# VectorE's ratio at the head of each step of the factor pipeline, and routing weights turned and expanded by short one-pass products

## The reference, cut to what matters

```python
# decay mixing, per batch and channel, over time
decay = exp(-exp(w)) * (0.5 + 0.5 * tf)            # tf from cond, one number per batch
ek, ekv = exp(min(k, 30)), exp(min(k, 30)) * v
nf, df = forward scans of ekv, ek  (a = a * decay + ekv_t; b = b * decay + ek_t)
nb, db = the same scans in reverse
euk = exp(min(u + k, 30))
y = sigmoid(x) * (nf + nb - ekv + euk * v) / max(df + db - ek + euk, 1e-8) * (0.8 + 0.2 * tf)
# routed low rank layer, per token
h = silu(y @ rw1.T + rb1);  logits = (h @ rw2.T + rb2)[:, :16] + gates
coeff = softmax over the two largest logits, at their places, else 0      # 16 experts
xa = y @ A.T                                        # 16 experts x rank 16 = 256
out = x + (y @ W.T + bias) + (xa * coeff[expert]) @ B
```

## Time and profile before

| | us |
|---|---|
| median of 3 runs | 688.93 (688.32 to 689.98) |
| the profiled execution's own time | 688.6 |
| its span, first to last instruction | 686.6 |
| TensorE busy | 598.7 (87%) |
| VectorE busy | 526.6 (77%) |
| GpSimd busy | 368.1 (54%) |
| ScalarE busy | 357.1 (52%) |

### The profile page before, as it was taken

One profiled execution on the slowest core, in us unless ns is written; L12 is line 12 of the kernel. 1 busy time (PEld: TensorE's weight loads), 2 busy tenths in 40 slices (PEclk: granted clock), 3 DMA queues, 4 the chain that ended last, 5 costly groups with the idle time before them and its releaser, 6 DMA issues.

```text
span 686.6 us, 7030 instructions
## 1 busy us (share of the span) xinstructions
PE 598.7 (87%) x2626; PEld 490.1 (71%) x2626; DVE 526.6 (77%) x573; ACT 357.1 (52%) x418; POOL 368.1 (54%) x183
## 2 busy tenths in 40 slices
PE   0153588989999937999999999999999999999997
PEld 0132466768878825887888878888888888888886
DVE  7999999999999999998899797979897532021202
ACT  4777789785656666655655554656465420011000
POOL 1789997867868876647544753565465501000100
PEclk9976799989999978999999999999999999999999
DMA  5323476522945831234423360427132402040022
GB/s 190 122 90 121 124 254 205 194 100 71 215 107 121 203 113 64 74 113 160 141 73 113 109 198 32 153 63 242 33 116 84 124 29 66 27 153 1 25 67 76
DMA packets 33169, 78.42 MB, mean 114 GB/s; under 512 B 4720, under 2 KB 4848, under 8 KB 33136
## 3 DMA queue, kind: packets, MB, share of 16 engines
q1 hardware_dynamic: 30832, 73.79, 33.2%
q0 software_dynamic: 2304, 4.20, 3.8%
HBM read 57.00 MB, written 20.97 MB: 114 GB/s over the span
## 4 chain that ended last, share of the span: by engine, by line
PE 49%; DVE 25%; POOL 16%; issue 7%; ACT 1%; DMA 1%; SPq 0%; DVEq 0%; POOLq 0%; ACTq 0%
PE acc L925 15%; PE acc L927 15%; PE acc L926 15%; DVE mix L713 5%; POOL mix L602 4%; POOL kv L580 4%; POOL yr L586 4%; DVE yr L747 3%; DVE mix L708 3%; DVE eu L723 3%; DVE kv L718 2%; DVE xo L754 2%; POOL y_lo L612 2%; DVE mix L734 2%; PE acc L936 1%
## 5 line engine op out<-in xcount | busy, mean ns | idle before, releaser
L925 PE MATMUL acc<-y_hi,wa_hi 128*128 128x512 f32 x640 | 258.5, 404 | 59.7 <-POOL y_lo L612 52.7
L926 PE MATMUL acc<-y_lo,wa_hi 128*128 128x512 f32 x640 | 255.3, 399 | 0.0
L927 PE MATMUL acc<-y_hi,wa_lo 128*128 128x512 f32 x640 | 254.8, 398 | 0.0
L925 PEld LDWEIGHTS acc<-y_hi,wa_hi 128*128 128x128 f32 x640 | 124.1, 194 | 89.3 <-POOL y_lo L612 54.1
L927 PEld LDWEIGHTS acc<-y_hi,wa_lo 128*128 128x128 f32 x640 | 123.8, 194 | 26.7
L926 PEld LDWEIGHTS acc<-y_lo,wa_hi 128*128 128x128 f32 x640 | 124.2, 194 | 25.6
L602 POOL TENSOR_TENSOR mix<-mix,kv 128x1024 f32<-128x1024 f32 x31 | 74.3, 2397 | 75.7 <-DVE mix L692 59.4
L754 DVE SCALAR_TENSOR_TENSOR xo<-acc,bias_sb,xo 128x512 f32<-128x512 f32 x64 | 46.4, 735 | 75.2 <-PE acc L927 75.2
L612 POOL TENSOR_TENSOR y_lo<-yr,y_hi 128x1024 fp32r<-128x1024 f32 x31 | 74.3, 2398 | 50.2 <-ACT y_hi L402 50.2
L625 POOL TENSOR_TENSOR wx_lo<-xa,wx_hi 128x512 fp32r<-128x512 f32 x16 | 20.9, 1329 | 129.3 <-ACT wx_hi L470 129.3
L580 POOL TENSOR_TENSOR kv<-mix,kv 128x1024 f32<-128x1024 f32 (+1 forms) x32 | 75.4, 2356 | 5.3 <-DVE mix L734 5.3
(11 more groups left out here) (98 smaller groups left out, 738.3 us busy)
## 6 DMA issues: line engine op xcount, KB each, us to landing
kv<-f_cm SPq DMA_DIRECT2D x32, 512.0 KB, 3.6
yr<-x_cm SPq DMA_DIRECT2D x32, 512.0 KB, 3.4
out<-xo SPq DMA_DIRECT2D x64, 256.0 KB, 4.2
xo<-x_cm SPq DMA_DIRECT2D x64, 256.0 KB, 3.9
out<-xo POOLq DMA_DIRECT2D x16, 256.0 KB, 6.8
xa<-w_base SPq DMA_DIRECT2D x5, 512.0 KB, 3.5
xo<-w_base SPq DMA_DIRECT2D x3, 512.0 KB, 5.7
xo<-w_router_a SPq DMA_DIRECT2D x2, 480.0 KB, 3.6
```

What stands on the lines that cost most here:

```text
L925: nc.tensor.matmul(out_ap, wh, yh, start=start, stop=False)
L926: nc.tensor.matmul(out_ap, wh, yl, start=False, stop=False)
L927: return nc.tensor.matmul(out_ap, wl, yh, start=False, stop=stop)
```

## The change

VectorE's `ratio` moves from the middle of a step to its head and multiplies the inverse with the sigmoid; GpSimd's `gate_n` then multiplies the summed numerator with that, and its result is y. GpSimd's sum is written over the numerator, so that the buffer of k is free sooner. ScalarE's order changes with it: `exp_uk` and `sigmoid_r` come to the head of the step. The groups 0 and 1 take the same places in a step as the later ones, with G = 1 in steps 11 to 13. The routing weights are no longer repeated to 512 columns: high and low parts of the 16 weights, twice side by side (`cat`, 64 columns), are turned by four fp32r products (`turn`), copied by ScalarE (`copy_turned`), and expanded to 128 rows by two products of 512 columns with a constant 0/1 matrix (`spread`). `ident` and `expand` are loaded into a free buffer and copied to fp32r by ScalarE in step 3 (`constants`). `u_g` and its copy go away; `split_wx` on GpSimd comes after `split_lo`.

```diff
+        cat = nc.alloc_sbuf_tensor_at("cat", [P, TPG, 2, 2 * E], fp32r, offset=fan_at)
+        cat_t = nc.alloc_sbuf_tensor_at("cat_t", [4 * E, N], fp32r, offset=fan_at + 4 * N)
+        ident_r = sb("ident_r", [P, P], fp32r)
+        expand_r = sb("expand_r", [4 * E, P], fp32r)
...
-        (AFTER_FWD, AFTER_FWD_NUM, AFTER_RATIO, AFTER_BWD_DEN, AFTER_P2, AFTER_SUM, AFTER_BWD_NUM) = range(7)
-        hidden_at = {(CB, AFTER_BWD_NUM): 0, (CB + 3, AFTER_SUM): 1}
-        silu_at = {(CB + 1, AFTER_FWD): 0, (CB + 3, AFTER_BWD_NUM): 1}
-        routing_at = {(CB + 1, AFTER_BWD_DEN): 0, (CB + 4, AFTER_FWD): 1}
-        weigh_at = {(CB + 1, AFTER_P2): 0, (CB + 4, AFTER_RATIO): 1}
...
+        (AFTER_RATIO, AFTER_FWD, AFTER_FWD_NUM, AFTER_BWD_DEN, AFTER_SUM, AFTER_BWD_NUM) = range(6)
+        evacs_at = {(CB + 2, AFTER_RATIO): (0, 1), (CB + 2, AFTER_FWD): (1, 3), (CB + 2, AFTER_FWD_NUM): (3, 5),
+                    (CB + 2, AFTER_BWD_DEN): (5, 6), (CB + 2, AFTER_BWD_NUM): (6, 7), (CB + 3, AFTER_RATIO): (7, 8),
+                    (CB + 4, AFTER_BWD_NUM): (8, 10), (CB + 5, AFTER_FWD): (10, 12), (CB + 5, AFTER_FWD_NUM): (12, 13),
+                    (CB + 5, AFTER_BWD_DEN): (13, 14), (CB + 5, AFTER_SUM): (14, 15),
+                    (CB + 5, AFTER_BWD_NUM): (15, 16)}
...
         def first_step(G):
-            return CB + 4 * G
+            return CB + 4 * G if G != 1 else CB + 3
...
-        tasks_at = {first_step(G) + q: (G, q) for G in range(SPLIT, GROUPS) for q in range(3)}
+        tasks_at = {first_step(G) + q: (G, q) for G in range(GROUPS) for q in range(3)}
...
-                    sp.wait_ge(gated, g - 1)
+                    sp.wait_ge(y_ready if g - 2 in HALVED else n_ready, g - 1)
...
-                    act.wait_ge(n_ready, g - 1)
+                    act.wait_ge(y_ready, g - 1)
                 nc.scalar.activation(den_of(g), kv[:, g % 2, :], ACT.Exp).then_inc(ek_ready, 1)
 
             def exp_uk(g):
                 act.wait_ge(k_in[g % 2], 16 * (g // 2 + 1))
                 if g:
-                    act.wait_ge(y_ready, g)
-                nc.scalar.activation(eu[:], kv[:, g % 2, :], ACT.Exp, bias=u_f[:, g:g + 1]).then_inc(euk_ready, 1)
+                    act.wait_ge(ratio_ready, g)
+                nc.scalar.activation(eu[:], kv[:, g % 2, :], ACT.Exp, bias=u_sb[:, g % CB:g % CB + 1]).then_inc(euk_ready, 1)
...
+            def copy_turned(G):
+                act.wait_ge(turned, G + 1)
+                nc.scalar.activation(cat_t[:], acc[0:4 * E, banks[G][0], :], ACT.Copy).then_inc(cat_t_ready, 1)
...
-                routed = G >= 0
-                late_split = held(s - 1)
-                new = chunks_at(hi_steps, s)
-                z_of = {CB: 0, CB + 3: 1}.get(s, G if q == 0 else -1)
+                late_split, late_sigmoid = held(s - 1), held(s - 2)
+                if q == 1:
+                    sigmoid_z(G)
+                    if s < UNITS:
+                        sigmoid_r(s)
+                    exps()
+                if s < UNITS:
+                    exp_uk(s)
                 if q == 1:
                     copy_xa(G)
-                if s < UNITS:
+                if s - 1 in HALVED:
+                    split_late_hi(s - 1)
+                    scale_end_den(s)
+                    split_hi(s - 1)
+                if s < UNITS and q != 1 and not late_sigmoid:
+                    sigmoid_r(s)
+                if s < UNITS and s - 1 not in HALVED:
                     if s == 0:
                         act.wait_ge(recip_ready, 1)
                     scale_end_den(s)
                 if q == 1:
                     exp_gap(G)
-                if s == CB + 1:
-                    copy_xa(0)
-                if s == CB + 4:
-                    exp_gap(1)
-                    copy_xa(1)
-                if s < UNITS:
-                    if s - 1 in HALVED:
-                        split_late_hi(s - 1)
-                    scale_end_num(s)
-                if 0 < s <= UNITS and not late_split:
+                if 0 < s <= UNITS and not late_split and s - 1 not in HALVED:
                     split_hi(s - 1)
                 if q == 1:
-                    split_wx(G)
+                    copy_turned(G)
+                if s < UNITS and q != 1 and not late_sigmoid:
+                    exps()
                 if s < UNITS:
-                    exp_uk(s)
-                if s == CB + 4:
-                    split_wx(1)
+                    scale_end_num(s)
                 if s + 1 < UNITS:
                     exp_k(s + 1)
-                if s == CB + 1:
-                    exp_gap(0)
                 for n in chunks_at(hi_mid_steps, s):
                     weights_hi(n)
+                if s == 3:
+                    constants()
                 if s in part_steps:
                     for p in range(part_steps[s][0], part_steps[s][1]):
                         drain_part(p)
-                if z_of > 0:
-                    low_rows(z_of)
-                if s < UNITS:
+                if q == 1:
+                    split_wx(G)
+                if s < UNITS and late_sigmoid:
                     sigmoid_r(s)
-                if z_of == 0:
-                    low_rows(z_of)
-                if z_of >= 0:
-                    sigmoid_z(z_of)
-                if s < UNITS or z_of >= 0:
                     exps()
-                if s == CB + 1:
-                    split_wx(0)
+                if q == 0:
+                    low_rows(G)
                 if s < UNITS:
                     if s == 0:
                         act.wait_ge(gains_ready, 2)
                     inverse(s)
-                for n in new:
+                for n in chunks_at(hi_steps, s):
...
+            def n_of(g):
+                return kv[:, g % 2, :] if g in HALVED else num_of(g)
...
-                nc.gpsimd.tensor_tensor(kv[:, g % 2, t], num_of(g)[:, t], kv[:, g % 2, t], ALU.add).then_inc(n_ready, 1)
+                nc.gpsimd.tensor_tensor(n_of(g)[:, t], num_of(g)[:, t], kv[:, g % 2, t], ALU.add).then_inc(n_ready, 1)
 
             def gate_n(g):
                 pool.wait_ge(n_ready, g + 1)
-                pool.wait_ge(sig_ready, g + 1)
+                pool.wait_ge(ratio_ready, g + 1)
                 t = slice(0, N if g in HALVED else T)
-                nc.gpsimd.tensor_tensor(yr[:, g % 2, t], kv[:, g % 2, t], yr[:, g % 2, t], ALU.mult).then_inc(gated, 1)
-
-            def late_half(g):
+                nc.gpsimd.tensor_tensor(yr[:, g % 2, t], n_of(g)[:, t], yr[:, g % 2, t], ALU.mult).then_inc(y_ready, 1)
...
-                    late_half(s - 1)
+                    sum_late(s - 1)
                 if 0 < s <= UNITS:
                     sum_n(s - 1)
+                if s - 1 in HALVED:
+                    gate_late(s - 1)
...
-                if q == 1:
-                    split_wx(G)
                 if 0 < s <= UNITS and not late_split and s - 1 not in HALVED:
                     split_lo(s - 1)
                 for e in tiles(adds_at, s, AFTER_LO):
                     add_out(e)
                 for n in chunks_at(lo_late_steps, s):
                     weights_lo(n)
-                if s in (CB + 1, CB + 4):
-                    split_wx((s - CB) // 4)
+                if q == 1:
+                    split_wx(G)
...
-                dve.wait_ge(gated, g + 1)
-                t = slice(0, N if g in HALVED else T)
-                nc.vector.scalar_tensor_tensor(out=yr[:, g % 2, t], in0=eu[:, t], scalar=limit_f[:, g:g + 1],
-                                               in1=yr[:, g % 2, t], op0=ALU.min, op1=ALU.mult).then_inc(y_ready, 1)
+                dve.wait_ge(sig_ready, g + 1)
+                nc.vector.scalar_tensor_tensor(out=yr[:, g % 2, :], in0=eu[:], scalar=limit_f[:, g:g + 1],
+                                               in1=yr[:, g % 2, :], op0=ALU.min, op1=ALU.mult).then_inc(ratio_ready, 1)
...
-                for a in range(2):
-                    fan_out(a)
-
-            def fan_out(a):
...
+                nc.vector.tensor_tensor(second_hit, first_hit[:, :, :], second_hit, ALU.add).then_inc(route, 1)
+                twice = second_hit.unsqueeze(2).to_broadcast([P, TPG, 2, E])
+                routed_to(11 + 2 * TPG)
+                nc.vector.tensor_copy(cat[:, :, :, 0:E], twice).then_inc(route, 1)
+                routed_to(12 + 2 * TPG)
+                nc.vector.tensor_tensor(cat[:, :, :, E:2 * E], twice, cat[:, :, :, 0:E].bitcast(fp32),
+                                        ALU.subtract).then_inc(cat_ready, 1)
...
                 if ending:
                     evacuate(ended, 3)
                     evacuate(ended, 4)
-                if q == 1 and routed:
+                if 0 < s <= UNITS:
+                    ratio(s - 1)
+                first_groups(s, AFTER_RATIO)
+                if q == 1:
                     silu(G)
                 if s == 0:
                     scale_e(s)
                     p1(s)
                 if s < UNITS:
```

(55 more changed lines are left out.)

78 lines of the change are left out of this document (32 added, 46 removed).

## The result

| | before | after |
|---|---|---|
| median, us | 688.84 (688.12 to 689.98, 7 runs) | 683.66 (682.26 to 686.04, 7 runs) |
| profiled execution: own time, span | 688.6, 686.6 | 682.46, 680.4 |
| TensorE, VectorE busy | 598.7, 526.6 | 591.8, 520.8 |

The ratio is 0.9928, 95% interval 0.9915 to 0.9941: 5.2 us faster by the medians, where 7.6 were forecast; 683.66 is inside the range on record and 2.4 us above the forecast of 681.3. The runs of the changed kernel are spread over 3.8 us, those of before over 1.9. The profiled execution is one of the faster ones: its span is 6.2 us shorter than before, not 5.2.

A forecast was written before the change was run, and what follows sets the result against it. Bound by VectorE's factor pipeline until logits(2), then TensorE's stream. Terms 5.5 - 1.5 - 1.7 + 5.3 - 0.6 + 1.4 - 0.8 = 7.6 us gave 681.3 us from 688.93, range 674 to 687.

The forecast's parts named there:

- Head 16: Start of the ratio heading step 16, at the old forward scan's place: reached 5.5 us earlier, 248.7 instead of 254.16.
- The pipeline's step: VectorE's factor steps: 13.48 us back to back against 14.36, about 0.8 us less in each of steps 1 to 8.
- ScalarE late in step 5: ScalarE, with two weight chunks and two drains, hands exp_uk and the sigmoid late, delaying backward_den: 0.4 us lost.
- steps 9 to 15: Factor steps with groups 0 and 1: waits and fan_out shortened, against later weigh and evacuations; net gain 1.3 us.
- The clock: TensorE's clock may fall after idling 2.8 us before logits(2): costs 0 to 3.3 us, 1.7 taken.
- The stream: TensorE from logits(2) to the end: +5.3 turned weights, -0.6 extra wait, +1.4 late waits, -0.8 evacuation.
- The two late waits: TensorE's waits behind logits(2), for VectorE's evacuation (0.6 us) and unit 23 (0.8 us), go: 1.4 us gained.
- The clock holds: Rival at logits(2): the wait does not lower TensorE's clock, time 679.6 us; chance 0.27.
- The pipeline keeps its period: Rival: GpSimd or ScalarE sets 14.3 us in most steps, the 5.5 shrinks to about 1, time 685.8; chance 0.15.
- the port: Rival: GpSimd blocks VectorE's scale_e in steps 9 to 15, 0.8 us seven times, time 686.9; chance 0.05.
- The turned weights come late: Rival: ScalarE's copy takes 3 us, each of six groups loses 1 us, time 687; chance 0.08.
- Sigmoid waits for its load: Rival: x loads land late for the sigmoid, delaying backward_den; slower, about 694 us if 1 us late; chance 0.08.

The follow-up runs named there:

- second profile: The unedited changed kernel measured again beside the kernel before: median 684.19 us, ratio 0.9927; the profiled execution has a span of 685.4 us.
- router edit: Changed kernel with high parts of router chunks 4, 6, 8 moved from the end of ScalarE's steps 2, 3, 4 to the middle of the next: 684.56 us.
- fill: Changed kernel with nine products of block 1 moved ahead of logits(2) and six of block 2 ahead of turn(2): 683.5 us, ratio 0.9935.
- order only: Changed kernel's new order of steps with the old fan_out and old spread: 687.23 us, ratio to the kernel before 0.9986.
- weigh later: Changed kernel with weigh of groups 0 and 1 one scan later, behind backward_den: 685.15 us, ratio to the kernel before 0.9942.
- fill at G = 0, 1, 2: Changed kernel with products moved ahead of logits at G = 0 and 1 as well as G = 2: 684.82 us, ratio to the kernel before 0.9933.
- all three edits: Changed kernel with products moved ahead of logits(2) and turn(2), router chunks later, and weigh of groups 0 and 1 later: 681.12 us, ratio 0.988.

## Why the prediction was right, and where it was not

**The total** came out nearer than its terms, by luck. In the profile of the changed kernel the span is 6.2 us shorter than before, against 7.6 forecast. Head 16 gave 4.15 us less than forecast; 0.4 less lost from there to logits(2), 1.7 counted for the clock and not paid in that execution, and 0.6 more from the stream made up for 2.7 of them.

**The pipeline's step** was right: 13.48 us were counted and 13.43 measured in steps 1 to 3, with no wait before L717 or L753. So was the forecast that nothing is paid in step 0 beyond a small term: head 1 is 0.4 us earlier, not later.

**Head 16 reached 5.5 us earlier** is the step that failed: it came 1.35 us earlier in the first profile of the changed kernel and 2.1 us later in the second, and the prediction's own sign of being wrong, waits of backward_den for its end column, is there. Up to step 9 the prediction had 4.2 us, and 2.96 came (2.61 in the second profile). The 0.4 us for "ScalarE late in step 5" should have been 3.4: 1.91, 0.58, 0.17 and 0.70 us of backward_den waiting in steps 4 to 7. Step 0 (0.4 gained, not lost) and the eight steps (7.1 us by their bare length of 13.43, not 6.4) made up for part of it, and of the 0.4 counted for GpSimd there is no sign. The list of ScalarE was counted by its work, and its waits were left out: 2.94 and 0.89 us for chunks of weights and 1.02 and 1.55 us for stores of partial products. In the old order there was slack ahead of the sigmoid for these; in the new one the end column stands behind it. That the router edit took the waits of steps 4 and 5 away and gained 1.2 us or more by step 9 shows this part.

In steps 9 to 15 the prediction had +1.3 and got -1.6. It counted 2.2 us of waits for TensorE: 0.5 and 1.1 in weigh of G = 0 and 1, and 0.6 in the last evacuations of G = 1. Measured were 5.0: none and 1.41 in weigh, and 3.6 in the evacuations of G = 0 (0.30, 1.80, 1.07, 0.39), where none was counted. The 2.8 us too little are nearly the whole of the 2.9 that are missing. In the second profile these steps lost 4.7 us, with 4.6 in weigh and 3.2 for x. What makes TensorE late there stays open: in the first profile its own work was late by wx_lo (2.30 us) and its clock was at 0.69 from 150 to 155 us, in the second its clock fell behind logits(0), and no experiment separates these.

**Logits(2)**: 16.5 us after the head were counted, 16.03 measured; scale_e waited 0.42 us for exp_k, not 0.8.

**The clock** was put midway between two rows, 0 to 3.3 us. The runs show both ends. Without a fill, waits up to 2.43 us before logits(2) left it up; behind 2.98 and 3.15 us logits(3) came 73.0 and 72.9 us later instead of 71.4; behind 3.45, 3.52 and 3.67 us they came 74.5 us later, 3.1 us lost, which is near the bound. The Trainium skill ("TensorE: Matmul & The Clock Gate", Part 1) has the same mechanism, activity releasing a throttled default. The trace agrees: in each profile the clock came up from 0.50 to 1.00 while TensorE worked through the twenty products ahead of logits(2). Whether the middle, 1.7, is a fair mean is not shown: of the changed kernel there are two profiles, with 0 and 1.6 us lost.

The wait before logits(2) is not a measure of what was gained ahead of it. With head 16 within 0.12 us of the same place it was 2.12 us (order only), 3.67 (router) and 3.15 (weigh later). What differed is where in the twenty products the clock came up: near 265.4, 262.4 and 263.4 us. Sooner means that TensorE is done sooner and waits longer. So that the clock hid the gains of the router edit and of the later weigh is not shown: in their profiles head 16 was no earlier than in the first profile of the changed kernel.

**The stream** was right in sum, 5.3 us by its four terms and 5.9 measured. Turned weights: counted from start to start and above 0.227 us for every product behind, turn, spread and the restarts take 0.97 us of a group in the changed kernel and 1.79 in the order-only kernel, 0.82 less; six groups make 4.9, and 5.3 - 0.6 = 4.7 was predicted. Evacuate(G, 2) moved down: the groups differ by 0.53 us only, and the missing 0.3 lies 25 to 28 us behind logits, where three weight loads in a row are late, two of them waiting 0.21 and 0.28 us for the evacuation. That is the -0.8 of the prediction, at the place that it named (26.8 us behind logits); it came to 3.7 - 4.9 = -1.2, and only beside the shorter stream. The two late waits of before cost more than their length: logits(2) to (3) and (3) to (4) took 72.82 and 73.26 us instead of 71.93, 2.2 us for waits of 0.60 and 0.83, where 1.4 was predicted. TensorE's weight loads had waited 1.02, 0.29 and 1.25 us in these two groups, which fits the length lost better than the idle time of the products.

**The rivals.** "The clock holds" is what the first profile of the changed kernel shows and the second does not. "The pipeline keeps its period" named a shrunken gain of about 1 us at head 16, and that size came, but not its mechanism: the period did fall, and the gain was lost in waits. Of the port there is no sign where the rival had it: the scales of steps 9 to 16 took 0.74 to 0.78 us. Behind logits(2) three of them took 1.80, 1.58 and 1.79 us, where VectorE has time. "The turned weights come late" holds in the order of before and not in the new one. "Sigmoid waits for its load" did not occur.

**Open.** The runs of the changed kernel are spread over 3.8 and 5.5 us. Its two profiles, 680.4 and 685.4 us of span, differ by 3.45 us at head 16, of which 3.1 arise in steps 9 to 15, and by 1.6 us of clock behind logits(2). That is the whole difference, but what comes first in steps 9 to 15 was not settled: the second profile has lower clocks (0.66 from 115 to 120 us, 0.71 from 135 to 140), longer waits in weigh and waits for x. Nor was an edit made that keeps the stores of partial products out of ScalarE's way.

## What to carry to other kernels

When a wait is taken out of a loop, count the other engines' lists with their waits for transfers, not by their work alone: what now stands ahead of the next handover inherits them. A wait of TensorE can cost more than its length, here up to 3.1 us by the clock behind it, and its length depends on TensorE's own clock ahead of it as well as on what it waits for. Where the runs of one kernel are spread as wide as the effect, one profile of each kernel is not enough: here the changed kernel alone has two patterns of waits, and either is easily taken for the work of an edit. Two halves of a change can be worth nothing or less alone: put the small products where the engine that copies between them is free.

## What the runs showed of the hardware beyond what was expected

- Four fp32r products of 128 columns take 0.24 us from start to start of the next (0.06 each), against 0.11 for each of the sixteen instructions of the fp32 spread (1.70 us from start to start of the next in the order-only kernel).
- The granted clock fell behind logits(2) after waits of 0.90 us (fill at G = 0, 1, 2) and 1.01 us (all three edits, 0.78 from 270 to 275 us), and stayed at 1.00 after 2.43 us in the changed kernel, so the length of the last wait alone does not decide it. In the second of these the clock had come up near 262.0 us, in the last near 264.6.
- TensorE's idle time before a product understates a wait within its stream: before the change, products that had waited 0.60 and 0.83 us lengthened their groups by 0.89 and 1.33 us, and the weight loads ahead of them had waited 1.02 and 1.25 us.
